# First expert step: rows transposed in two types, and a chain of four VectorE instructions in place of one

## The reference

```python
x = L0_attn_x                                   # 8 x 512 x 256, float32
xn = _layernorm(x, axis=-1)
x = x + _L0_attn_ref(xn, ...) + _L0_ffn_ref(xn, ...)

# _L0_ffn_ref: mixture of 8 experts, two of them for each token, 256 -> 1024 -> 256
logits = xn @ router_w + router_b
keep = one_hot(top_k(logits, 2)).sum(-2) > 0
gating = softmax(where(keep, logits, -1e30))
h = relu(einsum('td,edh->eth', xf, w1) + b1)
y = einsum('eth,ehd->etd', h, w2) + b2
out = einsum('etd,te->td', y, gating)
```

## Time and profile before

| | |
|---|---|
| median of 3 runs | 963.66 us (963.28 to 963.79) |
| profiled execution, its own time | 962.66 us |
| its span, first to last instruction | 960.5 us |
| mean granted TensorE clock | 0.984 |
| PE busy in the span | 94% |
| VectorE busy | 86% |
| ScalarE busy | 77% |
| GpSimd busy | 51% |

### The profile page before, as it was taken

One profiled execution on the slowest core, in us unless ns is written; L12 is line 12 of the kernel. 1 busy time (PEld: TensorE's weight loads), 2 busy tenths in 40 slices (PEclk: granted clock), 3 DMA queues, 4 the chain that ended last, 5 costly groups with the idle time before them and its releaser, 6 DMA issues. The chain is left out here.

```text
span 960.5 us, 27552 instructions
## 1 busy us (share of the span) xinstructions
PE 901.5 (94%) x7684; PEld 874.9 (91%) x7684; DVE 821.9 (86%) x2171; ACT 739.9 (77%) x1983; POOL 494.6 (51%) x699
## 2 busy tenths in 40 slices
PE   4899799899999999999947999999999999999996
PEld 4788789889999999999947999999999999999996
DVE  5876699998888888888846999999999999999995
ACT  4445799889999999999935777777777777677773
POOL 5220013236565555555443666666666666666663
PEclk9999799999999999999987999999999999999999
DMA  4879433344444445444314222222212223222220
GB/s 147 324 276 311 146 78 94 108 124 136 135 134 141 142 136 150 138 133 135 101 46 165 38 39 43 40 41 41 33 29 43 47 46 48 43 44 35 34 24 1
DMA packets 69867, 95.33 MB, mean 99 GB/s; under 512 B 15549, under 2 KB 48960, under 8 KB 69696
## 3 DMA queue, kind: packets, MB, share of 16 engines
q1 hardware_dynamic: 52800, 77.97, 26.4%
q0 software_dynamic: 17024, 16.88, 11.1%
HBM read 62.91 MB, written 35.53 MB: 102 GB/s over the span
## 5 line engine op out<-in xcount | busy, mean ns | idle before, releaser
L1007 ACT ACTIVATE weights_qkv<-weights_qkv,low 128x256 f32<-128x256 f32 (+1 forms) x512 | 240.3, 480 | 1.4 <-DVE low L818 1.4
L1419 ACT ACTIVATE hid<-ps_experts,b_s 128x256 f32<-128x256 f32 x312 | 130.9, 473 | 115.4 <-PE ps_experts L1486 92.2
L1305 POOL DMA_INDIRECT out<-y,target x78 | 149.2, 1912 | 110.5 <-DVE y L1385 94.2
L829 DVE TENSOR_TENSOR pt<-ps_attend,pt 128x512 fp32r<-128x512 f32 (+1 forms) x256 | 158.5, 620 | 39.2 <-ACT pt L1020 26.1
L1097 PE MATMUL ps_attend<-pt,v_m 128*80 128x256 f32 (+7 forms) x1536 | 187.0, 271 | 2.3 <-DVE inv_t L842 1.0
L1502 PE MATMUL ps_experts<-w_hi,h_hi 128*128 128x256 f32 x624 | 175.5, 281 | 1.1 <-DVE h_lo L1352 1.1
L1486 PE MATMUL ps_experts<-xgt_hi,w_hi 128*128 128x256 f32 x624 | 173.3, 278 | 1.7 <-DVE xgt_lo L1343 1.7
L1097 PEld LDWEIGHTS ps_attend<-pt,v_m 128*80 128x80 f32 (+3 forms) x1536 | 170.7, 161 | 4.2 <-issue 4.2
L1486 PE MATMUL ps_experts<-xgt_hi,w_lo 128*128 128x256 f32 x624 | 173.2, 278 | 0.0
L1486 PE MATMUL ps_experts<-xgt_lo,w_hi 128*128 128x256 f32 x624 | 173.0, 277 | 0.0
L1502 PE MATMUL ps_experts<-w_lo,h_hi 128*128 128x256 f32 x624 | 172.4, 276 | 0.0
(11 more groups left out here) (165 smaller groups left out, 2007.9 us busy)
## 6 DMA issues: line engine op xcount, KB each, us to landing
weights_qkv<-in_w SPq DMA_DIRECT2D x15, 1024.0 KB, 6.7
qk_hi<-weights_qkv SPq DMA_DIRECT2D x16, 512.0 KB, 4.7
qk_lo<-weights_qkv SPq DMA_DIRECT2D x16, 512.0 KB, 5.7
q_st<-qk_hi SPq DMA_DIRECT2D x128, 64.0 KB
k_st<-qk_hi SPq DMA_DIRECT2D x128, 64.0 KB
weights_qkv<-in_x SPq DMA_DIRECT2D x8, 512.0 KB, 4.7
xn_rows<-weights_qkv SPq DMA_DIRECT2D x8, 512.0 KB, 5.3
k_st<-qk_lo SPq DMA_DIRECT2D x64, 64.0 KB
```

Of the source, the lines that this page charges most:

```text
L829: v.tensor_tensor(lo[:, f:l], ps[:, bank_t[h], 0:l - f], hi[:, f:l].bitcast(F32), ALU.subtract).then_inc(s_plo, 1)
L1007: ins = act.activation(wt[:, ring, at_tile(i)], wt[:, ring, at_tile(i)], ACT.Exp, bias=low[:, ring, i:i + 1], scale=-1.0, accum_out=total[ ...
L1305: pool.indirect_dma_start(out_tokens, bass.IndirectOffsetOnAxis(ap=target[:, h:h + 1], axis=0), y[:, h], None, bounds_check=T - 1, oob_is_ ...
L1419: ins = act.activation(hid[:, n % 2, j], ps[:, bank_h[n], j * ROWS:(j + 1) * ROWS], ACT.Relu, bias=b1[:, ds(e * FC + 2 * n + j, 1)])
```

## The change

For step 0 alone, the rows are transposed twice: by the four fp32r transposes as before, and by four more transposes in float32 into PSUM bank 7. VectorE makes the low part of the rows as before, but without letting PE go; then it copies bank 7 to SBUF (the first half of `hid`, not yet in use), subtracts this copy from bank 4, multiplies the difference by 2 to the 20th and adds it to the low part. The last of these four instructions increments `s_xlo`. Two semaphores are new: `s_words` (incremented by PE) and `s_apart` (incremented by VectorE, and waited for by VectorE itself). The other 38 steps are as before.

```diff
+        s_words = sem("s_words", "pe")
+        s_apart = sem("s_apart", "v")
...
-        bank_h, bank_t, bank_y = (0, 1, 2, 3), 4, (5, 6)
+        bank_h, bank_t, bank_y, bank_words = (0, 1, 2, 3), 4, (5, 6), 7
...
                 lo_of_w1(0, first, 0)
-                lo_of_rows(0)
+                apart = hid[:, 0].rearrange("p j n -> p (j n)")
+                low_rows = xt_lo[:].rearrange("p c n -> p (c n)")
+                v.wait_ge(s_xhi, 1 + START)
+                v.tensor_tensor(low_rows, ps[:, bank_t, :], xt_hi[:].rearrange("p c n -> p (c n)").bitcast(F32),
+                                ALU.subtract).then_inc(s_apart, 1)
+                v.wait_ge(s_words, 1 + START)
+                v.tensor_copy(apart, ps[:, bank_words, :]).then_inc(s_apart, 1)
+                v.wait_ge(s_apart, 2 + START)
+                v.tensor_tensor(apart, ps[:, bank_t, :], apart, ALU.subtract).then_inc(s_apart, 1)
+                v.wait_ge(s_apart, 3 + START)
+                v.scalar_tensor_tensor(out=low_rows, in0=apart, scalar=float(2 ** 20), in1=low_rows.bitcast(F32),
+                                       op0=ALU.mult, op1=ALU.add).then_inc(s_xlo, 1)
                 lo_of_w1(0, first, 1)
...
                 transpose_rows(0, 0)
+                for c in range(DC):
+                    for h in range(2):
+                        ins = pe.transpose(ps[:, bank_words, (c * 2 + h) * P:(c * 2 + h + 1) * P],
+                                           xg[:, 0, h, c * P:(c + 1) * P].bitcast(F32), g.ident[:])
+                ins.then_inc(s_words, 1)
```

## The result

The changed kernel takes 965.08 us in the median of 18 runs (963.96 to 966.99); the kernel before, run beside it, takes 962.94 (18 runs, 961.33 to 964.87). The ratio is 1.0024, with a 95% interval from 1.0017 to 1.0032, so +2.3 us (1.6 to 3.1; the medians themselves lie 2.14 apart): slower, by as much as was forecast.

A forecast was written before the change was run, and what follows sets the result against it. PE was taken to bound the kernel, with its early wait in step 0 passing to the end. VectorE's 2.03 us plus 0.05 at the stage's start, clock nothing, gave +2.08 on 963.66: 965.74, rounded to 965.8 us; range 964.2 to 966.9.

The forecast's parts named there:

- What bounds the kernel: Experts' stage: PE bounds it, without waits between 510 and 948 us, so a late first product delays the end equally.
- named signs of being wrong: Copy waiting for `s_words`, new PE wait, product spacing outside 0.11 to 0.12 us, end shift unlike first full-clock product's.
- Part 1: PE's four float32 transposes, step 0: end at about 509.6, hidden, cost nothing; uncovered they would cost 1.0 us.
- Part 2: VectorE ahead of `s_xlo`: copy, second subtraction, multiply-and-add add 2.03 us (1.77 to 2.4).
- rival E: VectorE's copy runs at the SBUF price: +1.8 us, 965.5; chance within the forecast's 0.37.
- Part 3: Later low parts of `w1` and `w2` on VectorE: delayed but hidden, by 1.8 us and more.
- Part 4: Start of the experts' stage: one more VectorE semaphore increment delays the first gather, 0.05 us (0 to 0.13).
- Part 5: PE's clock at layer 1: full speed again 3.6 us after the first product, so the term is nothing.
- rival B: Clock rises later than 3.6 us after PE resumes: 1.4 us cost 0.6, +2.7 us, 966.4; chance 0.24.
- Rival A: Clock rises at the same moment as before, 514.0, giving back 0.93: +1.15 us, 964.8; chance 0.28.
- Rival C: Four extra transposes bring full clock by layer 1's start, saving 1.6 us: +0.5, 964.2 us; chance 0.08.
- Rival D: Both kinds of transpose give the same words, the added difference is zero; forecast's time, chance within its 0.37.

The follow-up runs named there:

- transposes alone: Changed kernel with only the four float32 transposes kept, the low part made by one VectorE instruction as before: 962.89 us, ratio 1.0002 to the kernel before.
- chain off the path: Changed kernel with `s_xlo` incremented by the first subtraction, the other three VectorE instructions writing to unused `y`: 962.86 us, ratio 0.9998 to the kernel before.
- chain alone: Changed kernel without the float32 transposes, its four VectorE instructions kept, the copy reading bank 4: 966.18 us, ratio 1.0036 to the kernel before.
- chain made longer: Changed kernel with VectorE's copy and second subtraction done twice: 965.90 us, ratio 1.0037 to the kernel before.
- the filling in the wait: Changed kernel with six 128x512 products into an unused bank behind the float32 transposes, while PE waits for VectorE: 963.60 us, ratio 0.9998 to the kernel before.
- high parts first: Kernel before with each sum's four products needing only the rows' high part first, `s_xlo` awaited at the fifth: 961.93 us, ratio 0.9991.

## Why the prediction was right

- **What bounds the kernel.** Right: no wait is new, the wait in the last step is the same 1.1 us, and from step 2 on the shift stays (3.52 and 3.51). One of the named signs of being wrong did occur: the shift at the end is 0.4 us more than at the first landmark at full speed (3.13, step 1's transposes). That is no wait, but the wider distance between the products of one step.
- **Part 1, the transposes.** Right: they end 1.59 us after the fp32r ones start (1.6 forecast), and alone they cost nothing that could be measured (+0.2 and −0.2 us, each give or take 1, in the two kernels that have them without waiting for the chain).
- **Part 2, the chain.** Right to 0.02: 2.05 against 2.03 us. The copy from PSUM took 0.68, so the SBUF price of rival E is out.
- **Part 3, who is queued behind.** Right: with all of the work there but PE not waiting for it, the ratio is 0.9998 (0.9989 to 1.0008).
- **Part 4, one more increment at the start.** From SyncE's first issue to VectorE's cast it is 0.62 us instead of 0.53, so 0.09 and not 0.05. It is too small to be seen in a time.
- **Part 5, the clock.** A term of nothing agrees with the times (2.3 measured, 2.08 forecast; the interval leaves room for −0.5 to +1.0). In the median that is part luck: the term was taken because it lies between the other two outcomes, and no row showed how often each of them comes. It is not right for the profiled execution, where it was +0.75, as in rival B (+0.6), at the forecast price of 0.445 a us. In the profiles that share the start of the stage, full speed came 3.7 us after the first product (before), 5.4 (changed), 4.2 (transposes alone), 3.6 (chain off the path), 5.5 (chain alone) and 4.2 (chain made longer): no fixed delay, and no order by the length of the chain. The Trainium skill (TensorE: Matmul & The Clock Gate, Part 1) has the monitor that sets the clock run freely of the kernel; the lack of a fixed delay in these six is in line with it. That a half-speed stretch costs what was reckoned is shown by the filling in the wait.
- **Rival A**, the rise at the same moment, did not occur in the profile (518.1, not 514.1). **Rival C** named the right price with the wrong cause: four transposes alone don't bring full speed ahead of layer 1, six wide products behind them do. (By the Trainium skill, same page, Part 4, transposes do not count as products do. The runs don't speak against it, but four transposes take 1.07 us and six wide products 2.65, so kind and length are not told apart.) By time, A's 1.15 lies outside the interval of 1.6 to 3.1, forecast and B inside. **Rival D** names the forecast's time, so no time can tell it, and no run compares the words that the two transposes give.

The median came out at 965.08 and not at 965.8 mainly because the kernel before, in more runs, has a median of 962.94 and not 963.66. The step "I carry the difference over" added 1.00 us to the profiled execution on the strength of three runs.

Why the chain alone measured 3.5 us and the whole change 2.3, with paths equal to 0.01 us, can be read from the mean granted clock that each execution has on record. The changed kernel has nine executions at 0.985 (mean 964.31 us) and eight at 0.983 (966.17); the chain alone has one at 0.985 (964.31), six at 0.983 (965.99) and one at 0.981 (966.51). At the same clock the two agree within 0.2 us; the chain alone only fell more often on the lower one, which in eight executions can be chance. The step is as large as it should be: 0.002 of 960 us are 3.8 us at half speed, 1.7 us at the price of 0.445, against 1.9 measured.

The kernel before has 0.986 in 26 of the 77 executions that were timed beside the experiments (mean 961.82), 0.984 in 31 (963.33) and 0.982 in 12 (963.93). Read between these, it would take about 962.6 us at 0.985 and 963.6 at 0.983; the changed kernel lies 1.7 and 2.5 above, 2.1 in the mean. This is an estimate, as the clock is given to 0.001 and as a mean of the whole program. It agrees with 2.04 us for the chain, and leaves a few tenths for the clock. What decides on which clock an execution falls stays open.

## What to carry to other kernels

A short chain costs its full length where the bound engine stands still once and never waits again; look for that place before judging a change by the engines' busy shares. If the waiting engine is TensorE, the wait can cost twice, by its length and by a slower clock behind it. Here, independent products in the gap gave back the clock's part (2.5 us), though the wait stayed; the same kind of filling ahead of a wait of 1.7 us gave 0.9 us only; and an order that uses first what comes first brought the first product 0.7 us forward. Where an effect is below 0.3%, a distance between two instructions in the profile tells what the times can't.

## What the runs showed that was not expected

Products of 256 columns at full clock stand either 0.113 or 0.118 us apart, for many steps at a time. In the kernel before it was 0.118 up to about 519 us and 0.113 from there to the end of the stage; in the changed kernel 0.118 up to 533, in the kernel with high parts first up to about 540. I found no cause; a stretch of 96 products costs 0.4 us more at the wider distance.

The same stage of `attend`, untouched by any edit, began to run at full speed at different times. Windows of the kernel with the chain alone:

```profile
107.00:108.00 1.00, 0.38 (x4) 0.24 (x4) 0.85 (x4) 1.00 (x6) 0.00 (x0) 0.93 0.00 0
...
108.00:109.00 1.00, 0.94 (x8) 0.70 (x8) 1.00 (x6) 1.00 (x5) 0.00 (x0) 1.00 0.32 86
```

Here the clock was back at 107.1 us, where it came at 111.3 in the earlier trace rows and stayed at half until then. At 104.7 us the two kernels still stood within 0.05 us of each other; near 119 us this one was 1.25 us ahead, and its experts' stage began at 498.4 instead of 499.7. Seven profiles fall in two groups: where the rise came between 107 and 108 us (chain alone, chain made longer, high parts first) the experts' stage began at 498.3 to 498.5, and where it came at 111.3 or later (before, changed, transposes alone, chain off the path) at 499.7 to 500.1. So some 1.3 us, more than half of what this change costs, can come into a pair of profiles from 400 us upstream; that is why the shifts above are taken from the transposes of step 0, not from the start of the span.
